# Biases of two projections added by TensorE, token rows in eight places, router probabilities written once (first stage of a two-layer model)

## What is computed

```python
h = L0_tok_weight[x]
h = h + L0_attn(layernorm(h))     # linear attention, 8 heads, relu(q), relu(k); y = out @ Wproj.T + bproj
h = h + L0_ffn(layernorm(h))      # 32 experts: softmax(xn @ W_router + b_router), each expert takes its 512 best tokens
h = h + L1_attn(layernorm(h))     # softmax attention, causal
h = h + L1_ffn(layernorm(h))      # 8 experts, the best two of each token
```

## Time and profile before

| | |
|---|---|
| median of the runs | 2666.74 us |
| the profiled execution | 2664.6 us, span 2662.9 us |
| busy over the span: PE, DVE, ACT, POOL | 85%, 73%, 63%, 44% |
| busy in 202.6 to 222.2 us, one round: PE, DVE, ACT, POOL | 16.28, 17.03, 13.95, 11.03 of 19.60 us |
| granted TensorE clock over the span | 0.938 |

### The profile page before, as it was taken

One profiled execution on the slowest core, in us unless ns is written; L12 is line 12 of the kernel. 1 busy time (PEld: TensorE's weight loads), 2 busy tenths in 40 slices (PEclk: granted clock), 3 DMA queues, 4 the chain that ended last, 5 costly groups with the idle time before them and its releaser, 6 DMA issues.

```text
span 2662.9 us, 58077 instructions
## 1 busy us (share of the span) xinstructions
PE 2256.9 (85%) x16551; PEld 2003.8 (75%) x16551; DVE 1941.9 (73%) x8859; ACT 1681.3 (63%) x5240; POOL 1178.9 (44%) x1217
## 2 busy tenths in 40 slices
PE   4888878576667599999999999999999999999473
PEld 4777755455555488888888899999989899889463
DVE  4888856644444388888888988788798888888522
ACT  4776745222222377777777788888878788778253
POOL 7555300588888302222222234444436554454343
PEclk9999989777777799999999999999999999999787
DMA  2332310244444520000000155555537754773387
GB/s 79 95 84 80 88 39 1 50 73 78 75 72 74 102 54 26 26 27 29 25 25 25 32 135 151 155 150 152 151 96 223 221 157 112 213 205 105 110 259 216
DMA packets 282605, 271.30 MB, mean 102 GB/s; under 512 B 32795, under 2 KB 232057, under 8 KB 282288
## 3 DMA queue, kind: packets, MB, share of 16 engines
q1 hardware_dynamic: 231600, 195.90, 27.1%
q0 software_dynamic: 46080, 61.16, 10.2%
q10 hardware_dynamic: 4608, 10.52, 1.3%
HBM read 182.69 MB, written 86.84 MB: 101 GB/s over the span
## 4 chain that ended last, share of the span: by engine, by line
PE 48%; DVE 25%; POOL 12%; issue 8%; DMA 3%; SPq 2%; ACT 1%; DVEq 0%; POOLq 0%; ACTq 0%
POOL hbuf L816 7%; PE bank L2148 6%; PE bank L2061 6%; PE bank L2134 5%; PE bank L2069 5%; PE bank L2101 4%; PE bank L2109 3%; POOL xe L808 3%; PE bank L2060 3%; PE bank L2081 3%; PE bank L2083 3%; PE bank L2082 3%; DVE pr_place L1550 2%; DVE nmax L1532 2%; DVE pr_place L1543 2%
## 5 line engine op out<-in xcount | busy, mean ns | idle before, releaser
L856 POOL DMA_INDIRECT spread_rows<-kb,pos x256 | 249.2, 973 | 455.1 <-ACT pr_place L1069 318.1
L870 POOL DMA_INDIRECT zbuf<-pc,kb x232 | 232.4, 1002 | 265.3 <-DVE pc L1712 214.7
L1067 ACT ACTIVATE pr_place<-bank,nmax 128x128 f32<-128x128 f32 x512 | 188.5, 368 | 218.1 <-DVE nmax L1532 215.6
L2061 PE MATMUL bank<-xT,gT 128*128 128x256 f32 x1024 | 306.3, 381 | 0.0
L2069 PE MATMUL bank<-ident,pr_place 128*128 128x128 f32 x1536 | 254.6, 275 | 52.8 <-DVE pr_place L1550 52.4
L2069 PEld LDWEIGHTS bank<-ident,pr_place 128*128 128x128 f32 x1536 | 189.3, 141 | 139.7 <-DVE pr_place L1543 72.0
L1550 DVE COPY pr_place<-bank 128x384 f32<-128x384 f32 x512 | 281.4, 550 | 1.5 <-PE bank L2069 1.4
L2148 PE MATMUL bank<-wvo_part,x_part 128*128 128x512 f32 x768 | 268.3, 457 | 0.0
L1077 ACT ACTIVATE bank<-causal 128x384 f32<-128x384 f32 x512 | 253.4, 495 | 19.7 <-PE bank L2186 3.6
L1531 DVE TENSOR_REDUCE nmax<-bank 128x1 f32<-128x128 f32 x512 | 143.5, 280 | 158.6 <-PE bank L2061 156.8
L2134 PE MATMUL bank<-x_part,wqk_part 128*128 128x256 f32 x1536 | 245.5, 296 | 1.7 <-DVE x_part L1657 1.2
(11 more groups left out here) (322 smaller groups left out, 6276.8 us busy)
## 6 DMA issues: line engine op xcount, KB each, us to landing
pa<-bundle SPq DMA_DIRECT2D x186, 321.0 KB
wu_more<-bundle SPq DMA_DIRECT2D x62, 321.0 KB
junk<-zbuf SPq DMA_DIRECT2D x32, 512.0 KB
kb<-spread_rows SPq DMA_DIRECT2D x232, 65.0 KB
xrow<-xr SPq DMA_DIRECT2D x32, 320.0 KB, 2.5
hbuf<-h SPq DMA_DIRECT2D x32, 256.0 KB, 3.0
hx<-hbuf SPq DMA_DIRECT2D x64, 128.0 KB, 2.8
h3buf<-h SPq DMA_DIRECT2D x64, 128.0 KB
```

Source lines behind the costliest of these rows:

```text
L2061: pe.matmul(s2[:, P:3 * P], g[:, P:2 * P], xT3[:, p], start=False, stop=True, skip_group_check=True)\
```

## The change

The projection and the logits get their biases on TensorE. At the start DVE splits each bias into three bf16 parts that add up to it, puts part k into row k of a 128-row tile, zeros in the others (`three_parts`: 20 instructions, over `TG` = 4 copies side by side, `bproj3` with 512 columns and `brout3` with 128). A bf16 matmul of ones (`onesb`) with such a tile writes the bias into every row of a PSUM bank, and the matmuls of the projection and of the logits add to it (`start=False`). PE waits once, before its rounds, for the 20 steps and for `onesb`.

`add_bias`, `xb` and L1225 go. The residual is read straight from the gathered rows, which stay until h1 is made: `xg` has eight places, four in `vo_place` and four where `xb` was. A gather now waits for h1 of the group eight before it. `pg` goes: the probabilities are written once, into `xr`; POOL copies them from there into `pa`, and PE turns them from `pa`, so it waits for that copy and no longer for DVE.

```diff
         pc = sb("pc", [P, E0, P])
-        xb = pc[:, 0:4 * TG].rearrange("p (q j) c -> p q j c", q=4)
+        xg_more = pc[:, 0:4 * TG].rearrange("p (q j) c -> p q j c", q=4)
+        def xg_at(g):
+            return xg[:, g % 8] if g % 8 < 4 else xg_more[:, g % 8 - 4]
+        def probs_of(p):
+            return xr[:, p, :, C:ROW]
         sel = sb("sel", [P, 2, P])
...
                 q = 2 * w + p
+                if g >= 4:
+                    pool.wait_ge(gathered[w][p], 64 * (g // 4))
+                if g >= 8:
+                    pool.wait_ge(h1_ready, g - 7)
                 pool.tensor_copy(idst[:, q], ids[:, bass.ds(TG * g, TG)]).then_inc(idst_ready, 1)
                 for j in range(TG):
-                    pool.indirect_dma_start(out=xg[:, q, j], out_offset=None, in_=L0_tok_weight,
+                    pool.indirect_dma_start(out=xg_at(g)[:, j], out_offset=None, in_=L0_tok_weight,
                                             in_offset=bass.IndirectOffsetOnAxis(ap=idst[:, q, j:j + 1], axis=0))\
                         .then_inc(gathered[w][p], 16)
-            def add_bias(g, w, p, guard):
-                pool.wait_ge(gathered[w][p], guard)
-                if not isinstance(g, int) or g >= 4:
-                    pool.wait_ge(h1_ready, g - 3)
-                pool.tensor_tensor(xb[:, 2 * w + p], xg[:, 2 * w + p], bproj[:].unsqueeze(1).to_broadcast([P, TG, C]), ALU.add)\
-                    .then_inc(xb_ready, 1)
                 pool.nop(nofuse=True)
-                pool.tensor_copy(pa[:, bass.ds(g * TG, TG)], pg[:, p]).then_inc(pa_ready, 1)
+                pool.tensor_copy(pa[:, bass.ds(g * TG, TG)], probs_of(p)).then_inc(pa_ready, 1)
                     gather(2 * w + p, w, p)
-            for p in range(2):
-                add_bias(p, 0, p, 64)
                     for p in range(2):
-                        pool.wait_ge(xn_ready, 2 * i + p + 1)
-                        pool.wait_ge(xb_ready, 2 * i + p + 1)
                         gather(2 * (i + 2) + p, w, p)
-                if within(i + 1):
-                    for p in range(2):
-                        add_bias(2 * (i + 1) + p, 1 - w, p, 64 * (v + w + 1))
                 if within(i - 1):
...
+            def three_parts(row, out, width):
+                low = lg[:, 0].rearrange("p j e -> p (j e)")[:, 0:width]
+                part = lg[:, 1].rearrange("p j e -> p (j e)")[:, 0:width]
+                cut = junk[:, 0:width]
+                src = row[:]
+                for k in range(3):
+                    bias.done(dve.tensor_copy(cut, src))
+                    bias.wait()
+                    if k == 0:
+                        bias.done(dve.tensor_scalar(part, cut, ident[:, 0:1], None, ALU.mult))
+                    else:
+                        bias.done(dve.scalar_tensor_tensor(out=part, in0=cut, scalar=ident[:, k:k + 1], in1=part, op0=ALU.mult, op1=ALU.add))
+                    bias.done(dve.tensor_tensor(low, src, cut, ALU.subtract))
+                    bias.wait()
+                    src = low
+                bias.done(dve.tensor_copy(out[:].rearrange("p (j c) -> p j c", j=TG), part.unsqueeze(1).to_broadcast([P, TG, width])))
+                bias.wait()
+            bias = Steps(dve, bias_step)
+            three_parts(bproj, bproj3, C)
+            three_parts(brout, brout3, E0)
+            assert bias.n == BIAS_STEPS
             ROOT = 13
...
                 dve.wait_ge(lg_mm, g + 1)
-                steps.done(dve.tensor_tensor(lg[:, p], bank[4 * p + 3][:, 0:TG * E0].rearrange("p (j e) -> p j e", j=TG),
-                                             brout[:].unsqueeze(1).to_broadcast([P, TG, E0]), ALU.add))
+                sums = bank[4 * p + 3][:, 0:TG * E0].rearrange("p (j e) -> p j e", j=TG)
+                steps.done(dve.tensor_reduce(mx[:, p], sums, AX.X, ALU.max))
                 steps.wait()
-                steps.done(dve.tensor_reduce(mx[:, p], lg[:, p], AX.X, ALU.max))
-                steps.wait()
-                dve.tensor_tensor(lg[:, p], lg[:, p], mx[:, p].unsqueeze(2).to_broadcast([P, TG, E0]), ALU.subtract)\
+                dve.tensor_tensor(lg[:, p], sums, mx[:, p].unsqueeze(2).to_broadcast([P, TG, E0]), ALU.subtract)\
                     .then_inc(lg_sub, 1)
...
                     dve.wait_ge(pa_ready, g - 1)
-                    dve.wait_ge(pT_mm, g - 1)
-                dve.tensor_tensor(pg[:, p], lg[:, p], sm[:, p].unsqueeze(2).to_broadcast([P, TG, E0]), ALU.mult)
-                dve.tensor_tensor(xr[:, p, :, C:ROW], lg[:, p], sm[:, p].unsqueeze(2).to_broadcast([P, TG, E0]), ALU.mult)\
+                dve.tensor_tensor(probs_of(p), lg[:, p], sm[:, p].unsqueeze(2).to_broadcast([P, TG, E0]), ALU.mult)\
                     .then_inc(p_ready, 1)
             def round_steps(i):
-                return ROOT + 4 + (LN_STEPS + 8) * within(i - 1) + LN_STEPS * within(i + 2)
+                return ROOT + 4 + (LN_STEPS + 6) * within(i - 1) + LN_STEPS * within(i + 2)
...
             pe.wait_ge(prep_c, 6)
+            pe.wait_ge(bias_step, BIAS_STEPS)
+            pe.wait_ge(consts4, 11 + 3 * NK)
...
                 pe.wait_ge(x2T_ready, g + 1)
+                pe.matmul(bank[4 * p + 3][:, 0:TG * E0], onesb[:], brout3[:], start=True, stop=False, skip_group_check=True)
                 for j in range(TG):
                     ins = pe.matmul(bank[4 * p + 3][:, j * E0:(j + 1) * E0], x2T[:, p, j * P:(j + 1) * P], wrout[:],
-                                    start=True, stop=True)
+                                    start=False, stop=True, skip_group_check=True)
                 ins.then_inc(lg_mm, 1)
             def turn_probs(g, p):
-                pe.wait_ge(p_ready, g + 1)
-                pe.transpose(bank[4 * p + 3][:, 0:P], pg[:, p].rearrange("p j e -> p (j e)"), ident[:]).then_inc(pT_mm, 1)
+                pe.wait_ge(pa_ready, g + 1)
+                pe.transpose(bank[4 * p + 3][:, 0:P], pa[:, g * TG:(g + 1) * TG].rearrange("p j e -> p (j e)"), ident[:]).then_inc(pT_mm, 1)
...
                     ins.then_inc(oT_mm, 1)
+                    pe.matmul(bank[4 * p + 2][:, :], onesb[:], bproj3[:], start=True, stop=False, skip_group_check=True)
                 if within(i - 1):
...
                         ins = pe.matmul(bank[4 * p + 2][:, j * P:(j + 1) * P], oT[:, p, j * P:(j + 1) * P], wprojT[:],
-                                        start=True, stop=True)
+                                        start=False, stop=True, skip_group_check=True)
                     ins.then_inc(y_mm, 1)
```

More of the change, by code:

```diff
@@ L164, in lm_tower @@
         sm = sb("sm", [P, 2, TG])
-        pg = sb("pg", [P, 2, TG, E0])
+        bproj3 = sb("bproj3", [P, TG * C], BF16)
+        brout3 = sb("brout3", [P, TG * E0], BF16)
         pa = sb("pa", [P, NT, E0])
@@ L326, in lm_tower @@
         root_ready = sem("root_ready")
-        xb_ready = sem("xb_ready")
+        bias_step = sem("bias_step")
         xn_ready = sem("xn_ready")
@@ L463, in lm_tower @@
         NU = E0 // 4
+        BIAS_STEPS = 20
         NP = NG // 2
@@ L933, in first_norm @@
                     act.wait_ge(xT_mm, g - 1)
-                normalise(xn[:, p], xg[:, 2 * w + p], 2 + p).then_inc(xn_ready, 1)
+                normalise(xn[:, p], xg_at(g), 2 + p).then_inc(xn_ready, 1)
             def second_norm(g, p, i):
@@ L1212, in roots, with first_stats @@
                                          op0=ALU.mult, op1=ALU.mult).then_inc(root_ready, 1)
-            def first_stats(w, p, guard, steps):
-                dve.wait_ge(gathered[w][p], guard)
-                stats(xg[:, 2 * w + p], 2 + p, steps)
+            def first_stats(i, p, steps):
+                dve.wait_ge(gathered[i % 2][p], 64 * (i // 2 + 1))
+                stats(xg_at(2 * i + p), 2 + p, steps)
             def second_stats(g, p, steps):
@@ L1285, in one @@
                 if within(i + 2):
-                    first_stats(w, 0, 64 * (v + 2), steps)
+                    first_stats(i + 2, 0, steps)
                 if rear:
@@ L1290, in one @@
                 if within(i + 2):
-                    first_stats(w, 1, 64 * (v + 2), steps)
+                    first_stats(i + 2, 1, steps)
                 for p in range(2):
                     dve.wait_ge(y_mm, g0 + p + 1)
-                    dve.wait_ge(xb_ready, g0 + p + 1)
                     if rear:
@@ L1297, in one @@
                         dve.wait_ge(x2_ready, r0 + p + 1)
-                    dve.tensor_tensor(h1[:, p], bank[4 * p + 2][:, :].rearrange("p (j c) -> p j c", j=TG), xb[:, 2 * w + p], ALU.add)\
+                    dve.tensor_tensor(h1[:, p], bank[4 * p + 2][:, :].rearrange("p (j c) -> p j c", j=TG), xg_at(g0 + p), ALU.add)\
                         .then_inc(h1_ready, 1)
@@ L1306, in _ @@
             for p in range(2):
-                first_stats(0, p, 64, steps)
+                first_stats(0, p, steps)
             roots(2, 4, steps, None)
             for p in range(2):
```

(2 more changed lines are left out.)

## The result

The changed kernel takes **2642.52 us**, the median of four runs (2639.83 to 2645.81), beside 2666.73 us for the kernel before on the same chip (2664.40 to 2667.24). The ratio is **0.9911, 95% interval 0.9894 to 0.9929**: 24.2 us less, where 23.2 were forecast. The profiled execution took 2639.83 us, its span 2638.1, with a mean granted clock of 0.937.

The account below looks back on a forecast made before the run. DVE was taken as the bound, PE one short step behind. 18.1 + 5.0 - 1.2 - 1.1 + 2.4 = 23.2 us less, from 2666.7 to 2643.5 us; range 2639 to 2651.

Parts of the forecast that it names:

- The main term: Regular rounds, DVE: L1230's wait for POOL's sums goes, 18.1 us in twelve rounds; bounds 18.1 or 0.
- Probabilities once: Between h1 sum and statistics on DVE: one of two writes goes per group, 0.42 us a round, 5.0 in twelve.
- L1225 against the bias matmuls: Around the router's logits: 0.21 us saved on DVE, 0.30 lost to PE; about +0.1 a round, 1.2 in twelve.
- matmul of 128 columns: Router's bias on PE before the logits: taken as 0.085 us, between 0.054 and 0.113.
- The regular round: First stage, from one h1 sum to the next: a round takes 17.9 us.
- PE keeps up: Idle PE covers the shift before keys and values but for 0.1 us; 0.6 is left before the attention outputs.
- POOL's slack: Gathered rows landing before DVE wants them: slack of 1.9 us falls by 1.3 to 0.6.
- one late gather: Gather behind a POOL pause of 2.03 us: 1.1 us now shows, if such a pause comes again.
- rival 2: Gathers become the bound: one microsecond more in descriptors or landing gives 18.3 us, +0.4 a round, 2649; 6%.
- The start: First gathers no longer delayed by POOL's sums: 2.4 us back; splitting the biases on DVE costs nothing.
- The end of the stage: Rounds 14 and 15 and the tail: losses and gains together 0, bounds -1 and +1 us.
- Rival 5: TensorE clock in the first stage: a slow stretch, seen once behind idle PE, L1870 5.38 us for 3.69; 2%.

## Why the prediction was right

**The main term** was L1230's wait for POOL's reading sums, 18.1 us. It is shown from both sides: take POOL's reads away, or DVE's second SBUF operand, and the subtraction takes 0.29 us.

**Probabilities once**, 5.0 us: 19.59 becomes 19.17, 0.42 a round.

**L1225 against the bias matmuls**, forecast +0.1 us a round, was about -0.06. From the last wait of DVE before the outputs (196.06 before, 165.19 after) to the first logits it was 4.65 us and is 4.84: lost 0.19, not 0.30. From the first logits to the h1 sum it was 4.38, of which 1.41 was the hold, and is 2.72: saved 0.25, not 0.21. The mis-sized term is the matmul of 128 columns: I took 0.085, between two rows, and it is 0.055, a quarter of the 512-column one; the two waits of DVE, 0.63 and 0.30, stand for my 0.7 and 0.4. The two matmuls between the last output and the first logits add to 0.27, of which 0.19 shows. PE does not wait there; the other 0.08 is in shorter distances beside them: the four transposes ahead take 0.49 in place of 0.53 (168.20 to 168.69, before 199.06 to 199.59), and DVE starts 1.07 behind the first logit matmul in place of 1.12. Over twelve rounds the term was 1.9 us too dear. The two rows of before that stand nowhere above:

```profile
196.06 0.17 DVE L1273 TENSOR_SCALAR den<-bank 128x16 f32<-128x16 f32 x1 [0.29 <-PE bank L1892]
```

```profile
199.06 0.65 PE L1901 MATMUL bank<-ident,pr_place 128*128 128x128 f32 x4 [0.40 <-DVE pr_place L1282]
```

**The regular round** comes out: 19.59 - 1.41 - 0.42 - 0.06 = 17.70, measured 17.69, forecast 17.9 as a mean.

**PE keeps up**, with 0.25 us of idle before the keys and values (waiting for ACT), as forecast, and 0.34 before the attention outputs, where I had 0.6; that DVE comes 0.15 earlier explains part of it.

**POOL's slack** was the weak step. I gave one late gather 1.1 us. The expected one cost 2.0, a late landing 1.5, and the slow stretch of PE behind the first 1.1: 4.6 us. The expected one cost more because its last gather, issued at 260.24, reached DVE 3.13 us later and not 2.5, and because the slack was 0.44 us and not 0.6 (last gather at 168.55 plus 2.5, rows wanted at 171.49). The 4.41 us from issue to DVE's start at 226.03, beyond the 3.5 of the earlier trace rows, I had not allowed for. The mechanism is that of rival 2, in two rounds of twelve and not in all.

**The start** gave 1.7 us (51.27 to 49.60), not 2.4. "Nothing" for `three_parts` was wrong: DVE is idle there, but POOL, which prepares the first gather, is slowed beside its steps, by 0.66 us. In addition the round from the first to the second h1 sum took 17.01 us and not 16.52. **The end of the stage** lost nothing: the last h1 sum is 20.7 us earlier, the first transposes of the table 21.2, from 358.5 to 337.3.

So the twelve rounds gained 19.5 us where 20.8 were forecast (3.5 more lost to late rows, 1.9 won on the biases, 0.3 that I can't place), the start with its next round 1.2 for 2.4, the end 0.5 for 0: together 21.2 for 23.2. The profiled executions differ by 24.8; the missing 3.6 lie in stages whose code did not change, and I cannot name their cause; they are less than the spread of the four runs, 6.0 us. The medians differ by 24.2. That the total fits so well is partly luck.

**Rival 5**, the clock, got 2%, with the argument that the one slow stretch of this stage came behind a long idle time of PE and that the change only shortens those. The trace of before has a second one, which I overlooked, and PE was at work ahead of it (busy for all of 140 to 142 us):

```profile
143.00:144.00 1.00, 1.00 (x6) 0.50 0.00 0
```

On the first chip the forecast held all the same. On two of the four chips of the experiments the clock of the changed kernel and of its variants falls in most rounds of this stage, and the outcome there is "no change". The trace of one chip could not show this.

**A version that beats both?** By the rounds of the first chips, the router's bias on TensorE with POOL's sums kept has a round of 17.96 with the probabilities written twice; less 0.42 that is 17.54, under the changed kernel's 17.69. It was built with earlier gathers (the one with the sums kept) and ran only on a chip of the second kind, so whether it beats the changed kernel is open. One row there shows that the wait is not gone for other instructions: a product of two SBUF operands that began 0.3 us before POOL's sums ended took 0.48 us, not 0.29.

```profile
73.74 2.48 POOL L785 TENSOR_TENSOR pc<-pc,bproj 128x512 f32<-128x512 f32 x2
```

```profile
75.90 0.48 DVE L1277 TENSOR_TENSOR xr<-lg,sm 128x128 f32<-128x128 f32 x1
```

## What to carry to other kernels

When one DVE instruction of a line is far longer than its sisters, look at what GpSimd does at that moment. Here it waited (1.70 us in place of 0.29) when it read two SBUF operands while GpSimd read; moving one operand to PSUM was enough, and GpSimd's work could stay. A bias in a matmul's bank cost 0.215 us for 512 columns here and 0.055 for 128. When a round gets shorter, price the slack of its DMAs by the worst landing, not by the median. Where the clock falls, look first at what held PE up just before. And measure on more than one chip before a gain of 1% is believed.

## What was not expected

- Two of the chips take 2775 us where the others take 2662 to 2667, and a change that is worth 0.9% on one is worth nothing on another (1.0014 [0.9997, 1.0031]).
- DVE's small steps at the start lengthen what POOL does beside them: 0.5 to 0.7 us on the first gather. Which of the steps do it was not taken apart, but for the router's, which cost 0.03.
- POOL's pause of 2.03 to 2.04 us in place of 0.30 comes ahead of the 114th of the 128 gathers, in all fourteen traces, on every chip: at 271.48 us before, 252.05 after, 259.52 with the router's bias alone on PE, 320.24 in the changed kernel on the third chip. It goes with the count of gathers and not with the time: it is the 114th also where the gathers stand a round earlier in the program. I had treated it as something that might come again; it is certain, and only whether it is hidden was open.
